# Half products dealt between the last units of attention, and the order of small sums on VectorE, in a GNN and attention kernel

## The chip, the cores and the metric

The kernel runs on one core of one Trainium2 chip. The metric is the device time of one execution in microseconds (us), the median of three runs. The profile is that of one further execution.

## What is computed

Node features x (1024 x 512) pass a layer norm and a relu, then a graph convolution, four transformer layers and a second graph convolution. The layers are nearly all of the time:

```
for i in range(L):                       # L = 4
    a = _attn(_ln(h, ln2), cond, Wq[i], Wk[i], Wv[i], Wo[i])
    h = h + a
    u = _ln(h, ln3) @ geglu_w[i] + geglu_b[i]          # 512 -> 4096
    val, gate = jnp.split(u, 2, axis=-1)
    f = val * gelu(gate)
    h = h + f @ ffo_w[i] + ffo_b[i]                    # 2048 -> 512
# _attn: 16 batches; 64 queries (rows of h) and 256 keys and values (from cond) each, 8 heads of 64
```

## The kernel before

Each of the five engines has its own instruction list, written out by hand in Python functions; nothing is scheduled by a program. Order between engines is kept by semaphores: `x.wait_ge(sem, value)` in front of an instruction, `.then_inc(sem, 1)` behind one. A waiting instruction holds up all that stands behind it on its engine. TensorE is `pe` (PE in the profile), VectorE `dve` (DVE), ScalarE `act` (ACT), GpSimd `pool` (POOL).

**Split products.** Every float32 product is three matmuls: upper by upper part, upper by lower, lower by upper. The upper part of a tile is a rounded copy, made mostly by ScalarE (`..._high`), the lower part the rest, a subtraction on VectorE or GpSimd (`..._low`). `product` (L2347 to L2349) issues these three per piece of 128 rows; four pieces (KC) make a product of 12 matmuls.

**A layer's attention.** The 1024 rows are 8 groups of 128 (t = 0 to 7), two batches each. Per group, keys and values are each made by a seven-product scheme: `kv_step(t, kind, j)`, j = 0 to 6, 12 matmuls of 256 columns each (L2596 to L2599), into three PSUM banks. VectorE combines them: `kv_two` (L1977), `kv_five` (L1985, the "fifth step's sum"), `kv_late(.., 0 to 2)` (L2000). Step 4 waits for `kv_five`, step 6 for `kv_late(.., 1)` by

```
elif j == 6:
    pe.wait_ge(kv_sum, 5 * n + 4)
```

Each group has four units u (two heads each). A unit is `s_product` (scores), `maxima` (L2050), `exp_of`, `softmax` (the reciprocal, L2056), `normalise`, `p_transpose` (L2624), `pT_high` and `pT_low` (L2061), `pv_product` (L2643 to L2648) and `o_part` (L2038, sums halves of its result out of the one bank that the next `pv_product` needs). `value_units(t)` interleaves the values of group t with its first two units, `key_units(t)` the keys of group t + 1 with its last two. `o_low` (L2044) makes the lower part for the output product `wo_product(t - 1)`, whose result `residual` (L2068) adds to h; norm statistics follow, the reciprocal root on GpSimd (`rsqrt`), `z3_of` (L2075), four transposes on TensorE (`t3`, L2692), `x3_full` (ScalarE, L1295), `x3_high` (L1304) and `x3_low` (L2088 on VectorE, L866 on GpSimd): the input of the second half of the layer. In layer 0 ScalarE and GpSimd also split the conditioning blocks of the next group (`cond_block`, `cond_low`); step j of the keys waits for block j.

**Front of a layer.** The first four query tiles (use 0, then use 1) go through `first_t2` (transposes), `first_x2_full` (L2006), `first_x2_high` (ScalarE), `first_x2_low` (L2015) and `q_product(use, p)`, with the seven key steps of group 0 in between.

**End of the attention.** The last group has no keys to make. Products of the second half's first four steps (s = 0 to 3, value and gate v = 0, 1; `mlp_product(0, 0, s, v, r)`) are put in their place. A half product takes the first 256 or the last 256 of the 512 columns: tiles 0, 1 or 2, 3 of x3 (of tiles 4 to 7 for s = 2, 3). Step s = 3 uses the banks of s = 1. After step s comes `gelu(s)` on ScalarE and `mlp_step(s)` (L2197) on VectorE, which raises `ff_ok`. Then come `full_product` (L2716 to L2720) and the rest of the layer, in which TensorE doesn't stop.

## Time and profile before

| | us |
|---|---|
| three runs | 2416.61, 2417.24, 2417.92 |
| median | 2417.24 |
| profiled execution | 2417.82 |
| its span | 2416.0 |
| TensorE busy (14270 matmuls) | 2331.7 (97%) |
| VectorE busy | 1635.8 (68%) |
| ScalarE busy | 1244.2 (51%) |
| GpSimd busy | 1050.1 (43%) |
| chain that ended last: TensorE, VectorE, ScalarE, GpSimd | 78%, 10%, 7%, 2% |

Times in the rows are microseconds from the start of the span. Matmuls overlap: one of 256 columns lasts 0.28 us from its start to its end, but the next starts long before. Layer 0 begins at about 178 us; the shown rows are mostly of layer 2 (1275 to 1828 us), as layers 1 to 3 repeat to a tenth of a microsecond.

### The profile page before, as it was taken

What the parts mean: (1) busy time and instruction counts of PE and PEld (TensorE: products, weight loads), DVE (VectorE), ACT (ScalarE), POOL (GpSimd) and SP (SyncE); (2) the same over time, 40 slices, a digit from 0 to 9 for tenths busy, and PEclk for the clock granted to TensorE, in tenths of its full rate; (3) what the DMA queues carried; (4) which work ended last, traced back from release to release, by engine and by line L of the source; (5) the groups of instructions that cost most, each with busy time, mean ns of one, the idle gap of its engine ahead of it and who ended that gap; (6) DMA issues with size and microseconds to landing.
All of it is one profiled execution on the core that took longest, in us unless ns stands there. A gap on an engine that the chain in (4) does not pass through costs nothing.

```text
span 2416.0 us, 38420 instructions
## 1 busy us (share of the span) xinstructions
PE 2331.7 (97%) x14270; PEld 2047.1 (85%) x14270; DVE 1635.8 (68%) x3043; ACT 1244.2 (51%) x2585; POOL 1050.1 (43%) x714
## 2 busy tenths in 40 slices
PE   7898999999999999999999999999999999999999
PEld 5358898988888999988888999988888999888887
DVE  9975667686656666686656666686656666685554
ACT  9954666654333555654433555653333555553322
POOL 3126766646643322356542322356652322355530
PEclk9899999999999999999999999999999999999999
DMA  2033333312221433312231333312231333212230
GB/s 79 1 137 126 134 146 126 129 40 66 61 92 72 127 104 118 97 44 63 63 123 52 122 103 109 97 44 70 62 118 69 119 106 104 87 53 63 63 128 35
DMA packets 115880, 214.53 MB, mean 89 GB/s; under 512 B 9520, under 2 KB 71600, under 8 KB 113904
## 3 DMA queue, kind: packets, MB, share of 16 engines
q1 hardware_dynamic: 115408, 207.89, 26.2%
q10 hardware_dynamic: 288, 4.19, 0.4%
q8 instruction: 115, 1.88, 0.3%
q14 instruction: 69, 0.57, 0.1%
HBM read 176.13 MB, written 35.91 MB: 88 GB/s over the span
## 4 chain that ended last, share of the span: by engine, by line
PE 78%; DVE 10%; ACT 7%; issue 3%; POOL 2%; DMA 0%; DVEq 0%; SPq 0%; ACTq 0%; POOLq 0%
PE ps L2347 9%; PE ps L2348 9%; PE ps L2349 9%; PE ps L2596 8%; PE ps L2599 7%; PE ps L2598 7%; PE ps L2716 7%; PE ps L2720 7%; PE ps L2718 7%; PE ps L2624 2%; ACT z L1295 2%; PE ps L2646 1%; DVE oh_d L1698 1%; PE ps L2910 1%; PE ps L2648 1%
## 5 line engine op out<-in xcount | busy, mean ns | idle before, releaser
L2596 PE MATMUL ps<-cb,wk_hi 128*128 128x256 f32 x896 | 260.0, 290 | 18.4 <-DVE kv L2000 11.7
L2596 PE MATMUL ps<-wv_hi,cb 128*128 128x256 f32 x896 | 257.7, 288 | 8.9 <-DVE kv L1985 5.0
L2599 PE MATMUL ps<-cb,wk_lo 128*128 128x256 f32 x896 | 255.4, 285 | 0.0
L2598 PE MATMUL ps<-cb,wk_hi 128*128 128x256 f32 x896 | 255.4, 285 | 0.0
L2599 PE MATMUL ps<-wv_hi,cb 128*128 128x256 f32 x896 | 253.4, 283 | 0.0
L2598 PE MATMUL ps<-wv_lo,cb 128*128 128x256 f32 x896 | 253.4, 283 | 0.0
L874 POOL TENSOR_TENSOR f_lo<-ff,f_hi 128x512 fp32r<-128x512 f32 x128 | 169.0, 1333 | 171.2 <-ACT f_hi L1499 171.1
L823 POOL TENSOR_TENSOR v_lo<-kv,v_hi 128x512 fp32r<-128x512 f32 x96 | 124.5, 1298 | 257.5 <-ACT v_hi L1253 257.5
L2282 DVE TENSOR_TENSOR h<-h,ps 128x512 f32<-128x512 f32 x256 | 169.1, 683 | 65.4 <-PE ps L2349 64.8
L2347 PE MATMUL ps<-wf_hi,f_hi 128*128 128x512 f32 x512 | 199.2, 389 | 0.0
L2348 PE MATMUL ps<-wf_lo,f_hi 128*128 128x512 f32 x512 | 199.2, 389 | 0.0
L2349 PE MATMUL ps<-wf_hi,f_lo 128*128 128x512 f32 x512 | 199.2, 389 | 0.0
L2000 DVE TENSOR_TENSOR kv<-ps,kv 128x512 f32<-128x512 f32 x192 | 132.4, 690 | 90.6 <-PE ps L2599 86.8
L2596 PEld LDWEIGHTS ps<-cb,wk_hi 128*128 128x128 f32 x896 | 173.4, 194 | 23.7 <-DVE kv L2000 9.3
L2716 PE MATMUL ps<-xT_hi,wg_hi 128*128 128x512 f32 x480 | 187.2, 390 | 0.1
L2720 PE MATMUL ps<-xT_hi,wg_lo 128*128 128x512 f32 x480 | 186.8, 389 | 0.0
L2718 PE MATMUL ps<-xT_lo,wg_hi 128*128 128x512 f32 x480 | 186.7, 389 | 0.0
L2596 PEld LDWEIGHTS ps<-wv_hi,cb 128*128 128x128 f32 x896 | 171.5, 191 | 13.0 <-DVE kv L1985 6.8
L823 POOL TENSOR_TENSOR kT_lo<-kv,kT_hi 128x512 fp32r<-128x512 f32 x96 | 124.0, 1293 | 117.5 <-ACT kT_hi L1253 108.3
L2598 PEld LDWEIGHTS ps<-cb,wk_hi 128*128 128x128 f32 x896 | 173.8, 194 | 1.1
L2599 PEld LDWEIGHTS ps<-cb,wk_lo 128*128 128x128 f32 x896 | 173.6, 194 | 0.0
L2598 PEld LDWEIGHTS ps<-wv_lo,cb 128*128 128x128 f32 x896 | 171.7, 192 | 0.0
(376 smaller groups left out, 6886.1 us busy)
## 6 DMA issues: line engine op xcount, KB each, us to landing
cb<-cb_s SPq DMA_DIRECT2D x168, 512.0 KB, 4.6
stage<-in_pieces SPq DMA_DIRECT2D x256, 128.0 KB, 2.6
cb_s<-cb SPq DMA_DIRECT2D x56, 512.0 KB, 2.6
stage<-in_pieces SPq DMA_DIRECT2D x44, 512.0 KB, 3.7
stage<-in_condT SPq DMA_DIRECT2D x7, 1024.0 KB, 5.9
stage<-in_pieces SPq DMA_DIRECT2D x16, 256.0 KB, 3.3
at_s<-at_hi ACTq DMA_DIRECT2D x2, 2048.0 KB, 12.9
wo_raw<-in_pieces SPq DMA_DIRECT2D x8, 512.0 KB, 4.5
```

What stands on the lines that cost most here:

```text
L823: pool.tensor_tensor(kv_place(1, kind, *KV_LATER[n]), kv_temp(n), bits(kv_place(0, kind, *KV_LATER[n])), ALU.subtract).then_inc(kv_ok, 1)
L874: pool.tensor_tensor(f_lo[q % 2][:, c, half * HALF:(half + 1) * HALF], ff[:, s % 2, :], bits(f_hi[q % 2][:, c, half * HALF:(half + 1) * HA ...
L2282: dve.tensor_tensor(h[:, t, :], h[:, t, :], ps[:, down_bank(q, t), :], ALU.add)\
L2347: pe.matmul(bank, l_hi, r_hi, start=(first and i == 0), stop=False)
L2348: pe.matmul(bank, l_hi, r_lo, start=False, stop=False)
L2349: end = pe.matmul(bank, l_lo, r_hi, start=False, stop=(last and i == n - 1))
L2596: pe.matmul(to, l_hi, r_hi, start=(fresh and i == 0 and k == 0), stop=False, skip_group_check=True)
L2598: pe.matmul(to, l_hi, r_lo, start=False, stop=False, skip_group_check=True)
L2599: last = pe.matmul(to, l_lo, r_hi, start=False, stop=(k == 1), skip_group_check=True)
L2716: pe.matmul(ps[:, bank, :], hi[:, a, r], moving[0][:, n, :], start=(first and n == 0), stop=False, skip_group_check=True)
L2718: pe.matmul(ps[:, bank, :], hi[:, a, r], moving[1][:, n, :], start=False, stop=False, skip_group_check=True)
L2720: last = pe.matmul(ps[:, bank, :], lo[:, a, r], moving[0][:, n, :], start=False, stop=(n == 1), skip_group_check=True)
```

## The change

Instructions change places within their engines' lists; in addition two lower parts of x3 per layer (tiles 0 and 1) go from GpSimd (two instructions each) to VectorE (one each), and 36 matmuls per layer are added, since three products of 512 columns are issued as two of 256. Nothing is left out and no buffer is added. By part:

- Front of a layer: `q_product` takes a list of pieces and for p = 0 waits for one lower part of x2 per piece; `q_product(1, 0)` gives its first piece before key step 6. On VectorE `kv_late(0, KEYS, 1)` comes after the first lower part and the full part of tile 2.
- Groups: on VectorE `kv_five` comes before `q_low` in both halves of a group, `o_low` before the reciprocal. On ScalarE `q_high(t + 1, 0)` comes ahead of the conditioning blocks. For t = 0 `kv_late(.., 1)` of the values comes before the reciprocal.
- Last group and the start of the second half: other places for the half products on TensorE, with other waits; upper parts of x3 one or two units earlier on ScalarE (`x3_high(0)` after `pT_high(u)`, `x3_high(1)` at its old place, and in `key_units` `x3_full(5)`, `x3_high(2)`, `x3_high(3)` before `pT_high(u)`, `x3_high(4)` and `x3_high(5)` before `pT_high(u + 1)`); lower parts 0 and 1 among the value sums of group 7; `gelu(0)` before `x3_full(6)`; `mlp_step(0)` before `x3_low(6)`.

The diff without the parts on ScalarE and GpSimd that the list above gives in full (indentation cut):

```diff
@@ -1360,16 +1349,14 @@
...
             if last:
-                x3_high(0)
+                x3_high(1)
             if ahead:
...
                 o_high(GROUPS * l + t - 1)
-            if last:
-                x3_high(1)
-            elif t > 1:
+            if t > 1 and not last:
                 x3_full(t - 2)
@@ -1380,16 +1367,18 @@
...
             normalise(u)
+            if not last:
+                q_high(t + 1, 0)
             if ahead:
...
             if not last:
-                q_high(t + 1, 0)
                 kv_11_high(t + 1, KEYS)
             else:
+                x3_full(5)
                 x3_high(2)
-                x3_full(5)
+                x3_high(3)
             pT_high(u)
@@ -1402,13 +1391,11 @@
...
             else:
-                x3_high(3)
                 x3_high(4)
+                x3_high(5)
             pT_high(u + 1)
...
                 kv_high(t + 1, KEYS, 2)
-            else:
-                x3_high(5)
@@ -1516,9 +1503,9 @@
...
+        gelu(0)
         x3_full(6)
         x3_high(6)
-        gelu(0)
         down_high(0)
@@ -2096,35 +2083,45 @@
...
             if t:
-                q_low(t, 1)
                 o_part(u - 2, 2)
             kv_five(t, VALUES)
+            if t:
+                q_low(t, 1)
             kv_11_low(t, VALUES)
...
             kv_late(t, VALUES, 0)
+            if t == 0:
+                kv_late(t, VALUES, 1)
             softmax(u + 1)
-            kv_late(t, VALUES, 1)
             if t:
+                kv_late(t, VALUES, 1)
                 o_part(u - 1, 3)
+            if t == GROUPS - 1:
+                x3_low(0)
             kv_late(t, VALUES, 2)
+            if t == GROUPS - 1:
+                x3_low(1)
             maxima(u + 2)
+            if t == GROUPS - 1:
+                o_low(GROUPS * l + t - 1)
             pT_low(u + 1)
...
             u, last = UNITS * l + PAIRS * t + 2, t == GROUPS - 1
-            if last:
+            if t and not last:
                 o_low(GROUPS * l + t - 1)
             softmax(u)
-            if t and not last:
-                o_low(GROUPS * l + t - 1)
             if not last:
...
             if not last:
+                kv_five(t + 1, KEYS)
                 q_low(t + 1, 0)
-                kv_five(t + 1, KEYS)
+            else:
+                x3_low(2)
+                x3_low(3)
             if t:
@@ -2140,8 +2137,6 @@
...
             if last:
-                x3_low(2)
-                x3_low(3)
                 o_part(u, 2)
@@ -2169,13 +2164,12 @@
...
             first_x2_full(1, k)
-        for k in T2_ORDER[1][:2]:
+        first_x2_low(1, 0)
+        first_x2_full(1, 2)
+        kv_late(0, KEYS, 1)
+        for k in T2_ORDER[1][1:]:
             first_x2_low(1, k)
-        first_x2_full(1, 2)
-        for k in T2_ORDER[1][2:]:
-            first_x2_low(1, k)
-        for n in range(1, 3):
-            kv_late(0, KEYS, n)
+        kv_late(0, KEYS, 2)
         q_low(0, 0)
@@ -2292,11 +2286,11 @@
...
         add_bias(NT - 2)
+        mlp_step(0)
         x3_low(NT - 2)
...
         z3_of(NT - 1, GROUPS * l + NT - 1)
-        mlp_step(0)
         t_sums(0, (3,))
@@ -2665,17 +2659,22 @@
...
-        def q_product(use, p):
-
-            if p == 0:
-                pe.wait_ge(x2_ok, 2 * FIRST * l + FIRST * use + FIRST)
+        def q_product(use, p, places=range(KC)):
+
             if p == 0 and use == 0:
...
             r = slice(p * P, (p + 1) * P)
-            product(ps[:, FIRST_BANK[p], :], [(wq_hi[:, k, r], wq_lo[:, k, r], xT2_hi[:, k, :], xT2_lo[:, k, :])
-                                              for k in range(KC)]).then_inc(q_mm, 1)
+            for i in places:
+                k = T2_ORDER[use][i]
+                if p == 0:
+                    pe.wait_ge(x2_ok, 2 * FIRST * l + FIRST * use + i + 1)
+                last = product(ps[:, FIRST_BANK[p], :],
+                               [(wq_hi[:, k, r], wq_lo[:, k, r], xT2_hi[:, k, :], xT2_lo[:, k, :])],
+                               i == 0, i == KC - 1)
+            if places[-1] == KC - 1:
+                last.then_inc(q_mm, 1)
@@ -2805,33 +2804,37 @@
...
             pv_product(u - 2, t, 0)
+            if last:
+                pe.wait_ge(kv_sum, 5 * (kv_set(l, t, VALUES) + 1))
+                pe.wait_ge(w_ok, FIRST_PIECES + PIECES * l + 2)
+                pe.wait_ge(x3_ok, 2 + NT * l + 2)
+                mlp_product(0, 0, 0, 1, slice(0, 2 * P))
             if t:
...
                 kv_step(t + 1, KEYS, 3)
-            else:
-                pe.wait_ge(w_ok, FIRST_PIECES + PIECES * l + 2)
-                pe.wait_ge(x3_ok, 2 + NT * l + 2)
-                pe.wait_ge(full3_ok, NT * l + 6)
-                mlp_product(0, 0, 0, 0, slice(0, 2 * P))
             p_transpose(u)
...
                 kv_step(t + 1, KEYS, 5)
+            else:
+                pe.wait_ge(full3_ok, NT * l + 6)
+                mlp_product(0, 0, 0, 0, slice(0, 2 * P))
             pv_product(u - 1, t, 1)
...
             else:
-                mlp_product(0, 0, 0, 1, slice(0, 2 * P))
+                mlp_product(0, 0, 1, 0, slice(0, 2 * P))
                 pv_product(u, t, 2)
-                pe.wait_ge(x3_ok, 2 + NT * l + 4)
-                mlp_product(0, 0, 0, 0, slice(2 * P, HALF))
             p_transpose(u + 1)
...
             else:
+                mlp_product(0, 0, 1, 1, slice(0, 2 * P))
+                pe.wait_ge(x3_ok, 2 + NT * l + 4)
+                mlp_product(0, 0, 0, 1, slice(2 * P, HALF))
                 pv_product(u + 1, t, 3)
@@ -2845,9 +2848,11 @@
...
         first_t2(1, T2_ORDER[1][3:])
-        for j in range(5, BLOCKS):
-            kv_step(0, KEYS, j)
-        for p in range(PAIRS):
+        kv_step(0, KEYS, 5)
+        q_product(1, 0, range(1))
+        kv_step(0, KEYS, 6)
+        q_product(1, 0, range(1, KC))
+        for p in range(1, PAIRS):
             q_product(1, p)
@@ -2873,25 +2878,27 @@
...
+        mlp_product(0, 0, 0, 0, slice(2 * P, HALF)).then_inc(u_mm, 1)
         pe.wait_ge(o_part_ok, 2 + UNITS * l + UNITS - 1)
         t3(6)
-        mlp_product(0, 0, 0, 1, slice(2 * P, HALF)).then_inc(u_mm, 1)
-        mlp_product(0, 0, 1, 0, slice(0, 2 * P))
+        mlp_product(0, 0, 1, 0, slice(2 * P, HALF))
+        mlp_product(0, 0, 1, 1, slice(2 * P, HALF)).then_inc(u_mm, 1)
         wo_product(GROUPS * l + GROUPS - 1)
-        mlp_product(0, 0, 1, 0, slice(2 * P, HALF))
-        mlp_product(0, 0, 1, 1, ks=range(0, 3))
-        t3(7)
-        mlp_product(0, 0, 1, 1, ks=range(3, KC)).then_inc(u_mm, 1)
...
         mlp_product(0, 0, 2, 1, slice(0, 2 * P))
+        t3(7)
+
+        pe.wait_ge(ff_ok, 32 * l + 2)
+        for v in range(2):
+            mlp_product(0, 0, 3, v, slice(0, 2 * P))
         pe.wait_ge(x3_ok, 2 + NT * l + NT)
-        mlp_product(0, 0, 2, 0, slice(2 * P, HALF))
-        mlp_product(0, 0, 2, 1, slice(2 * P, HALF)).then_inc(u_mm, 1)
-        mlp_step(0, 0, 3)
+        for s in range(2, 4):
+            mlp_product(0, 0, s, 0, slice(2 * P, HALF))
+            mlp_product(0, 0, s, 1, slice(2 * P, HALF)).then_inc(u_mm, 1)
         full_product()
```

How the instructions stand, by engine. VectorE in `key_units` of a group with t from 1 to 6; the qbd rows are the query lower parts, L1985 (L1972 in the changed kernel) is the fifth step's sum, the rows from `wo_mm` down the residual and its norm statistics. Before:

```order
L2056 RECIPROCAL rinv<-rsum 128x2 [waits exp_ok]
L2044 TENSOR_TENSOR oT_lo<-o_full,oT_hi 128x512 [waits o_hi_ok]
L1977 TENSOR_TENSOR kv<-ps,kv 128x512 [waits kv_p1,step_mm]
L2038 TENSOR_REDUCE o_full<-ps 64x128 [waits o_ok,pv_mm]
L2038 TENSOR_REDUCE o_full<-ps 64x128
L2023 TENSOR_TENSOR qbd_a<-z,qbd_a 64x4x64 [waits qb_hi_ok]
L2023 TENSOR_TENSOR qbd_a<-z,qbd_a 64x4x64
L1985 TENSOR_TENSOR kv<-ps,kv 128x512 [waits kv_sum,step_mm]
L2068 TENSOR_TENSOR h<-h,ps 128x512 [waits wo_mm]
L1600 BN_STATS stats<-h 128x6 [waits h_att]
L1603 BN_AGGR mv<-stats 128x2 [waits ln]
L1606 TENSOR_SCALAR veps<-mv 128x1 [waits ln]
```

and in the changed kernel:

```order
L2031 TENSOR_TENSOR oT_lo<-o_full,oT_hi 128x512 [waits o_hi_ok]
L2043 RECIPROCAL rinv<-rsum 128x2 [waits exp_ok]
L1964 TENSOR_TENSOR kv<-ps,kv 128x512 [waits kv_p1,step_mm]
L2025 TENSOR_REDUCE o_full<-ps 64x128 [waits o_ok,pv_mm]
L2025 TENSOR_REDUCE o_full<-ps 64x128
L1972 TENSOR_TENSOR kv<-ps,kv 128x512 [waits kv_sum,step_mm]
L2010 TENSOR_TENSOR qbd_a<-z,qbd_a 64x4x64 [waits qb_hi_ok]
L2010 TENSOR_TENSOR qbd_a<-z,qbd_a 64x4x64
L2055 TENSOR_TENSOR h<-h,ps 128x512 [waits wo_mm]
L1587 BN_STATS stats<-h 128x6 [waits h_att]
L1590 BN_AGGR mv<-stats 128x2 [waits ln]
L1593 TENSOR_SCALAR veps<-mv 128x1 [waits ln]
```

The two query lower parts went from ahead of the fifth step's sum to behind it, and `o_low` (oT_lo) from behind the reciprocal to ahead of it.

TensorE in the second half's first steps, at the transposes of the last tile (`t3(7)`, ident,z). Before, they stand inside a product of step 1 of 512 columns, and `mlp_step(1)`'s `ff_ok` is waited for only before step 3. The transposes:

```order
L2347 MATMUL ps<-xT_hi,w_hi 128x512
L2348 MATMUL ps<-xT_lo,w_hi 128x512
L2349 MATMUL ps<-xT_hi,w_lo 128x512
L2692 MATMUL ps<-ident,z 128x128 [waits z3_ok]
L2692 MATMUL ps<-ident,z 128x128 x3
L2347 MATMUL ps<-xT_hi,w_hi 128x512
L2348 MATMUL ps<-xT_lo,w_hi 128x512
L2349 MATMUL ps<-xT_hi,w_lo 128x512
L2347 MATMUL ps<-xT_hi,w_hi 128x256 [waits x3_ok]
```

and, 48 matmuls of 256 columns later, the start of step 3:

```order
L2348 MATMUL ps<-xT_lo,w_hi 128x256
L2349 MATMUL ps<-xT_hi,w_lo 128x256
L2347 MATMUL ps<-xT_hi,w_hi 128x512 [waits ff_ok]
L2348 MATMUL ps<-xT_lo,w_hi 128x512
L2349 MATMUL ps<-xT_hi,w_lo 128x512
```

In the changed kernel the wait for `ff_ok` stands right behind them:

```order
L2341 MATMUL ps<-xT_hi,w_hi 128x256
L2342 MATMUL ps<-xT_lo,w_hi 128x256
L2343 MATMUL ps<-xT_hi,w_lo 128x256
L2691 MATMUL ps<-ident,z 128x128 [waits z3_ok]
L2691 MATMUL ps<-ident,z 128x128 x3
L2341 MATMUL ps<-xT_hi,w_hi 128x256 [waits ff_ok]
L2342 MATMUL ps<-xT_lo,w_hi 128x256
L2343 MATMUL ps<-xT_hi,w_lo 128x256
```

The products of steps 1 and 2 that stood between the transposes and the wait have moved ahead of the transposes or behind step 3's first halves.

## Rows read from the trace of the kernel before

**Rows 1.** The profile's page: the span.

```profile
span 2416.0 us, 38420 instructions
```

**Rows 2.** TensorE waits, whole span: line, releaser: us total, times, longest.

```profile
PE ps L2596 <- DVE kv L2000: 15.6, 8, 3.0
PE ps L2347 <- DVE oT_lo L2044: 10.2, 24, 1.1
PE ps L2596 <- DVE kv L1985: 8.4, 7, 3.5
PE ps L2643 <- DVE pT L2061: 5.6, 4, 1.4
...
PE ps L2596 <- POOL cb L803: 3.3, 6, 0.9
...
PE ps L2347 <- ACT z L1295: 2.3, 4, 0.6
...
PE ps L2643 <- DVE o_full L2038: 2.1, 4, 0.5
...
PE ps L2347 <- DVE xT_lo L2088: 1.6, 4, 0.4
```

**Rows 3.** TensorE timeline, front of layer 2: start, duration, operation [idle before].

```profile
1285.92 0.50 PE L2347 MATMUL ps<-xT_hi,wq_hi 128*128 128x512 f32 x1 [0.60 <-DVE xT_lo L2015]
...
1299.96 0.28 PE L2598 MATMUL ps<-cb,wk_hi 128*128 128x256 f32 x1
1300.08 0.28 PE L2599 MATMUL ps<-cb,wk_lo 128*128 128x256 f32 x1
1303.26 0.58 PE L2596 MATMUL ps<-cb,wk_hi 128*128 128x256 f32 x1 [2.90 <-DVE kv L2000]
```

**Rows 4.** TensorE, five longest stops: stretch, length, busy (count), clock, DMA.

```profile
203.00:215.00 12.00, 9.01 (x46) 0.86 0.00 1
243.00:255.00 12.00, 8.54 (x58) 0.86 0.60 220
760.00:772.00 12.00, 9.10 (x53) 1.00 0.01 1
1299.00:1311.00 12.00, 9.10 (x39) 0.72 0.00 0
1841.00:1853.00 12.00, 9.10 (x43) 0.86 0.01 2
```

**Rows 5.** Timeline of VectorE, keys of a middle group of layer 2.

```profile
1464.03 0.85 DVE L2023 TENSOR_TENSOR qbd_b<-z,qbd_b 64x256 fp32r<-64x256 f32 x2
1467.17 0.69 DVE L1985 TENSOR_TENSOR kv<-ps,kv 128x512 f32<-128x512 f32 x1 [2.29 <-PE ps L2599]
...
1472.65 0.69 DVE L2000 TENSOR_TENSOR kv<-ps,kv 128x512 f32<-128x512 f32 x1
```

**Rows 6.** Timeline of TensorE in the same group: output product, key step 6.

```profile
1462.69 0.50 PE L2347 MATMUL ps<-wo_hi,oT_hi 128*128 128x512 f32 x1 [0.30 <-DVE oT_lo L2044]
...
1473.39 0.39 PE L2596 MATMUL ps<-cb,wk_hi 128*128 128x256 f32 x1
```

**Rows 7.** Timelines of VectorE, ScalarE and TensorE, start of layer 2's second half.

```profile
1579.61 0.69 DVE L2068 TENSOR_TENSOR h<-h,ps 128x512 f32<-128x512 f32 x1 [0.41 <-PE ps L2349]
...
1587.02 0.75 DVE L2197 SCALAR_TENSOR_TENSOR ff<-ps,cols_sb,gel 128x512 f32<-128x512 f32 x1 [0.26 <-ACT gel L1449]
...
1583.64 1.51 ACT L1295 ACTIVATE z<-ps,cols_sb 128x128 f32<-128x128 f32 x4 [1.78 <-PE ps L2692]
...
1595.03 0.39 PE L2349 MATMUL ps<-xT_hi,w_lo 128*128 128x512 f32 x1
1595.26 0.39 PE L2716 MATMUL ps<-xT_hi,wg_hi 128*128 128x512 f32 x1
```

**Rows 8.** Timelines of VectorE and GpSimd, a middle group of layer 0.

```profile
328.04 2.96 DVE L2023 TENSOR_TENSOR qbd<-z,qbd 64x256 fp32r<-64x256 f32 x2
...
327.65 1.64 POOL L798 TENSOR_TENSOR t_s<-stage,t_s 128x512 f32<-128x512 f32 x1
```

More of the change, by code:

```diff
@@ L859, in _ @@
             for l in range(L):
-                def x3_low(t):
-                    r = slice(t % 4 * P, (t % 4 + 1) * P)
-                    pool.wait_ge(x3_hi_ok, NT * l + t + 1)
-                    for ks in (slice(0, 2), slice(2, KC)):
-                        last = pool.tensor_tensor(xT3_lo[t // 4][:, ks, r],
-                                                  z3[:, t, :].rearrange("p (k n) -> p k n", n=P)[:, ks, :],
-                                                  bits(xT3_hi[t // 4][:, ks, r]), ALU.subtract)
-                    last.then_inc(x3_ok, 1)
                 def f_low(q, s, half, c):
@@ L941, in value_units @@
                         cond_low(g, 3)
-                    if last:
-                        x3_low(0)
-                        x3_low(1)
                 def key_units(t):
@@ L1355, in value_units @@
                     pT_high(u)
+                    if last:
+                        x3_high(0)
                     exp_of(u + 1)
@@ L2116, in key_units @@
                     u, last = UNITS * l + PAIRS * t + 2, t == GROUPS - 1
-                    if last:
+                    if t and not last:
                         o_low(GROUPS * l + t - 1)
                     softmax(u)
-                    if t and not last:
-                        o_low(GROUPS * l + t - 1)
                     if not last:
@@ L2807, in key_units @@
                     pv_product(u - 2, t, 0)
+                    if last:
+                        pe.wait_ge(kv_sum, 5 * (kv_set(l, t, VALUES) + 1))
+                        pe.wait_ge(w_ok, FIRST_PIECES + PIECES * l + 2)
+                        pe.wait_ge(x3_ok, 2 + NT * l + 2)
+                        mlp_product(0, 0, 0, 1, slice(0, 2 * P))
                     if t:
```

## The prediction

> **What bounds the kernel now.** The page first: one core, span 2416.0 us [rows 1]. The profiled execution took 2417.82 us, of which 1.8 us lie around the span; it is 0.6 us above the median of the three runs, 2417.24. The sum below is a difference, so I add it to the median. A measurement of this kernel tells about 0.2% (4.8 us) from no change.
>
> Then the waits of TensorE over the whole span [rows 2]. Everything after the graph stage is a chain of matmuls, and what the change can give is the time in which TensorE stands still. Per layer these are few and repeat exactly: two at the front of the attention stage, one before each output product, a handful around the last group. The timeline of TensorE gives the price of a matmul back to back: 0.12 us at 256 columns [rows 3], 0.23 us at 512 [rows 7]. A half product (12 matmuls of 256) costs 1.44 us, a whole one 2.72 us, so dealing one whole as two halves costs 0.16 us. Last, the granted clock around the longest stops [rows 4]: of five stops, four are followed by a stretch at 1.2 instead of 2.4 GHz. The loss is (1 - clock) x 12 us: 1.7, 1.7, 0, 3.4 and 1.7 us, in all 8.5 us.
>
> **The change, part by part.**
>
> *Front of a layer, first query product.* It waits for all four lower parts of x2 (0.60 us idle) [rows 3]. Now it starts on the first; 0.6 idle and 0.15 of broken overlap go: 0.75 us in each of four layers, **-3.0**.
>
> *Front, key step 6.* TensorE stops 2.90 us before it [rows 3] because `kv_late(0, KEYS, 1)` stands on VectorE behind all lower parts of x2. Now that sum comes after one lower part and one transposed tile, and TensorE has three matmuls of the query product in between. VectorE then ends the sum about 2.75 us sooner, and TensorE waits 0.2 us: 2.75 in layers 1 to 3, **-8.3**, and their clock comes back, 3.4 + 1.7, **-5.0** [rows 4]. In layer 0, GpSimd still has to make the lower parts of the value weights and then of the next conditioning blocks, which follow a transfer; they let TensorE gain less. Bounds: 1.0 (that chain doesn't move) and 4.5 (all of it and the 1.7 of clock). I take **-2.2**, nearer to the lower end because the chain hangs on GpSimd work that moves little.
>
> *The fifth key step's sum ahead of the query lower parts.* This is the part that cuts both ways.
> In layer 0 the sum waits for query upper parts that ScalarE makes behind three conditioning blocks; the seven stops on L1985 are 8.4 us, 3.5 of it one stop [rows 2]. The long one is exchanged for a wait on the next sum: of 3.5 + 1.7 clock I count 3.2. Of the six others (5.0 us plus first-matmul losses) nearly all, 4.9. Together **-8.1**; bounds 4 and 11.
> In the groups t = 1 to 6 of every layer it costs. Before, the two lower-part instructions (0.88 us from start to start of the next) ran in 2.29 us in which VectorE waited for key step 2 [rows 5]. Now they stand behind the fifth step's sum, and from there VectorE has no gap: residual, statistics, `kv_11_low`, maxima, `pT_low`, `z3_of`, two more sums, until `kv_late(.., 1)` starts at 1472.65 and ends at 1473.34. Key step 6 needs it and starts at 1473.39 [rows 6], 0.05 us later, which is where it would start anyway. So the slack is about 0.1 us and the rest of 0.88 appears as a stop of TensorE: about 0.8 us in 18 groups. In layer 0 the same delay moves the residual, hence the reciprocal root on GpSimd, hence the lower parts of block 5, for which TensorE already waits (3.3 us in six stops) [rows 2]: 0.88 in six groups. **+19.7**. Bounds: 0 if the chain had slack, 24 x 0.98 if it had none and the first matmul is slow. I take it near the upper end, since the rows show start and end of the chain 0.05 us apart.
>
> *Output product.* It stops 0.3 us in groups 2 to 6 of each layer (20 of the 24 stops in 10.2 us) [rows 2, 6], as `o_low` stood behind the reciprocal. Now it stands ahead. With the broken overlap and the slow first matmul (0.50 instead of 0.40) I count 0.55 each: **-11.2**.
>
> *Last group and what follows.* Before, the stops there are 1.05 for oT_lo, 1.4, 0.6, 0.5 and 0.4: 4.0 us per layer [rows 2]. More half products are put between the units, and three whole products are split (36 extra matmuls, 0.5 us). Walking the changed order by the durations of the timeline, TensorE gets eight half products rather than five before the last output product, but the third product of values waits for `o_part`, which on VectorE now stands behind two lower parts of x3 that wait for ScalarE. If everything moved to VectorE ran alone, the last output product would end 0.7 us later than before for 4.3 us more work done.
> Then comes the step I weigh most. Half products of step 3 are put behind `t3(7)`, and wait for `ff_ok` 2, because steps 1 and 3 share banks. That value is written by `mlp_step(1)`. Its chain is unchanged: last output product, residual (1579.61), norm, `t3(7)`, `x3_full(7)` (starts 1583.64), upper part, gelu(1), `mlp_step(1)` (1587.02 + 0.75 = 1587.77) [rows 7]: 8.2 us. Before, TensorE had 11.2 us of other work behind `t3(7)`. Now only two half products stand between the output product and `t3(7)`, and nothing behind it, so TensorE stops from the end of the transposes (+4.0) to +8.2: **a new stop of 4.2 us per layer**. Six half products (8.7 us) follow, so the full product starts 16.9 us after the output product's end; before it was 1595.26 - 1579.61 = 15.7 [rows 7]. So +1.2, and with the 0.7 +1.9 per layer.
> Two of the moved instructions, `x3_low(0)` and `o_low`, now fall beside GpSimd's lower parts of v. The query lower parts show what that does: two take 0.85 us alone and 2.96 us beside GpSimd [rows 5, 8], 1.05 us more each. I count 0.9 for each of the two, since each delays what follows on VectorE: +1.8 per layer. Together 3.7 x 4 = **+14.8**; bounds 1.4 and 5 per layer.
> The Trainium skill (SBUF — State Buffer, section "SBUF: two separate sides") says more strictly that a VectorE instruction with two SBUF inputs and a GpSimd instruction exclude each other for their whole length, and whichever starts first keeps the other out. By that rule the moved `x3_low(0)` would wait for nearly all of a GpSimd subtraction; the row agrees with such a wait, its size per instruction being 1.05 us. Without that rule and that row the 1.8 would be 0.
>
> *Clock at the new stop.* No row has a stop of 4.2 us. The nearest, 2.9 to 3.5 us, lost 1.7 on average and 2.1 where they lost any [rows 4]. Being longer than all of these, I give it 2.1 each: **+8.4**; bounds 0 and 3.4 each.
>
> **Sum.** Gains 3.0 + 8.3 + 5.0 + 2.2 + 8.1 + 11.2 = 37.8. Costs 19.7 + 14.8 + 8.4 = 42.9. Net +5.1 us, 2422.3.
>
> **The rivals.**
> (a) *The VectorE chain after the fifth sum is not the limit.* If key step 6 starts on time in spite of the moved lower parts, 19.7 us go: 2402.6, faster. It decides once the chain has over 0.8 us of slack. For it: no stop of TensorE shows there now. Against: 0.05 us between the sum's end and the step [rows 5, 6].
> (b) *The stop after t3(7) is short.* If gelu(1) or the residual comes earlier than the old chain says, so that TensorE waits 2 us or less and keeps its clock, 4 x 2.2 + 8.4 go: 2405, faster. Against: every link of the chain has its old place behind `t3(7)`.
> (c) *No collisions with GpSimd.* Then 7.2 us go: 2415, no change. For it: half a microsecond of shift decides who starts first.
> (d) *The clock falls more often.* The two-microsecond wait before the third product of values, or a remainder in layer 0, add a slow stretch per layer as in the worst row (3.4 instead of 2.1), or the front's drops stay: +8 to +9, 2431.
>
> **How the numbers follow.** Forecast 0.5 (own range 2415 to 2429), (a) 0.1, (b) 0.1, (c) 0.15, (d) 0.15. Faster by over 0.2%: (a) and (b), 0.2. Same (2412.4 to 2422.1): (c) and a good third of the forecast, as 2422.3 lies on its edge, 0.35. Slower: 0.45. The range leaves out (a) and (b) and reaches down to 2411, under (c) and the forecast's own range, and up to (d): 2411 to 2431.
>
> **What would show it.** In the trace after: no stop of 2.9 us at the front of a layer and no slow clock there; no stop before the output products of groups 2 to 6; instead 24 stops of about 0.8 us at key step 6 (in layer 0, at step 5, 1.3 us); in each layer one stop of about 4.2 us behind the last transposes, released by the product of values and gelu on VectorE, with the clock at 1.2 GHz behind it in most layers; `x3_low(0)` or `o_low` ending about 1 us late beside GpSimd. Total idle before half products under 3 us per layer, or key step 6 without stops, would prove me wrong.

## The result, and the profile after

The changed kernel takes **2435.5 us** (median of 4 runs, 2432.8 to 2437.6) against 2417.0 of the kernel before on the same chip: ratio 1.0075, 95% interval 1.0062 to 1.0088. It is 18.5 us slower; the prediction said 5.1 slower, with a range that ended at 2431. The sign was right and every stop that was foretold is there; one place was overlooked, and the time lies outside the range.

The page of the changed kernel, its span and the busy times of the engines:

```profile
span 2433.5 us, 38716 instructions
...
PE 2337.2 (96%) x14414; PEld 2064.2 (85%) x14414; DVE 1662.9 (68%) x3051; ACT 1243.1 (51%) x2585; POOL 1038.4 (43%) x698
```

TensorE is busy 5.5 us more (before 2331.7), the span is 17.5 us longer. The waits of TensorE over the whole span (line, releaser: us in total, times, longest), against [rows 2]:

```profile
PE ps L2590 <- DVE kv L1987: 23.8, 35, 1.6
PE ps L2341 <- DVE ff L2191: 17.2, 4, 4.3
PE ps L2590 <- POOL cb L803: 8.8, 7, 1.4
PE ps L2637 <- DVE o_full L2025: 7.7, 4, 2.0
...
PE ps L2590 <- POOL wv_lo L782: 3.0, 1, 3.0
```

L1987 is `kv_late` (L2000 before): its longest stop has fallen from 3.0 to 1.6, but there are 35 of them instead of 8. The 10.2 us before the output products and the 8.4 on the fifth sum are gone. The 4.3 us stops on `ff_ok` 2 are there. Timeline of TensorE in layer 2 (start, duration, operation, in brackets the idle time before it and its releaser): key step 6 of the layer's front, key step 6 of a middle group, value step 6 of group 7, the third product of values of group 7, the first half product of step 3, the full product.

```profile
1310.18 0.39 PE L2590 MATMUL ps<-cb,wk_hi 128*128 128x256 f32 x1 [0.20 <-DVE kv L1987]
...
1477.85 0.39 PE L2590 MATMUL ps<-cb,wk_hi 128*128 128x256 f32 x1 [0.62 <-DVE kv L1987]
...
1559.61 0.39 PE L2590 MATMUL ps<-wv_hi,cb 128*128 128x256 f32 x1 [1.57 <-DVE kv L1987]
...
1576.02 0.35 PE L2637 MATMUL ps<-pT,v_hi 128*128 128x256 f32 x1 [1.97 <-DVE o_full L2025]
...
1598.68 0.58 PE L2341 MATMUL ps<-xT_hi,w_hi 128*128 128x256 f32 x1 [4.31 <-DVE ff L2191]
...
1610.00 0.40 PE L2715 MATMUL ps<-xT_hi,wg_hi 128*128 128x512 f32 x1
```

The 2.90 us at the front [rows 3] are 0.20 now. The third row is one that the prediction does not have. Its cause is on VectorE and GpSimd, same stretch:

```profile
1551.25 0.69 DVE L1972 TENSOR_TENSOR kv<-ps,kv 128x512 f32<-128x512 f32 x1 [0.31 <-PE ps L2593]
1551.86 4.52 DVE L2010 TENSOR_TENSOR qbd<-z,qbd 64x256 fp32r<-64x256 f32 x2
...
1558.88 0.68 DVE L1987 TENSOR_TENSOR kv<-ps,kv 128x512 f32<-128x512 f32 x1
```

```profile
1551.10 5.00 POOL L732 TENSOR_TENSOR w_lo<-stage,w_hi 128x1024 fp32r<-128x1024 f32 x2 [3.32 <-ACT w_hi L1298]
```

The two query lower parts of the last group, `q_low(7, 1)`, moved behind the fifth sum, run beside GpSimd's lower parts of the second half's weights (`up_low`) and take 4.52 us instead of 0.85. All that is queued behind them on VectorE is 3.7 us late, `kv_late(7, VALUES, 1)` too, for which value step 6 waits. In the kernel before, the same two lower parts (VectorE) had ended 0.16 us before GpSimd began (the second row is GpSimd):

```profile
1545.27 0.85 DVE L2023 TENSOR_TENSOR qbd<-z,qbd 64x256 fp32r<-64x256 f32 x2
...
1546.28 4.81 POOL L732 TENSOR_TENSOR w_lo<-stage,w_hi 128x1024 fp32r<-128x1024 f32 x2 [3.32 <-ACT w_hi L1311]
```

The granted clock in windows of 12 us around the stops (stretch, length, busy of each engine, then the clock as a share of 2.4 GHz, DMA share, GB/s): step 3 of layer 1; layer 2's value step 6, third product of values, and step 3; step 3 of layers 3 and 0.

```profile
1050.00:1062.00 12.00, 8.90 (x54) 8.90 (x55) 10.34 (x8) 5.33 (x11) 9.21 (x5) 0.72 0.29 87
1558.00:1570.00 12.00, 10.43 (x65) 9.86 (x65) 8.31 (x16) 9.18 (x25) 4.23 (x3) 0.86 0.13 37
1576.00:1588.00 12.00, 11.98 (x87) 11.91 (x88) 5.78 (x10) 5.79 (x12) 0.00 (x0) 0.86 0.01 1
1597.00:1609.00 12.00, 10.32 (x64) 10.32 (x65) 11.68 (x10) 4.70 (x9) 9.21 (x5) 0.72 0.29 87
...
2139.00:2151.00 12.00, 8.26 (x52) 8.26 (x53) 10.17 (x8) 5.73 (x12) 9.13 (x5) 0.72 0.29 86
...
505.00:517.00 12.00, 9.48 (x61) 9.48 (x62) 10.91 (x9) 5.36 (x10) 9.22 (x5) 0.72 0.31 88
```

A window at 0.86 holds 3.4 us at 1.2 GHz, one at 0.72 holds 6.8 (they differ from 1 by half the time at 1.2 GHz). Added over the layers (178 us to the end), the changed kernel's TensorE is at 1.2 GHz for 54 us, that of before for 17 [rows 4]; at half speed that costs at most 27 us against 8.5. It is less where TensorE stands still in part of the stretch: compared with matmuls at full clock, and with layers whose clock stays up, a stretch costs 2.1 to 2.7 us behind the 4.3 us stop, 1.2 behind the stop at value step 6 (from there to the third product of values 16.2 to 16.6 us in layers 1 to 3, 15.3 in layer 0) and 1.5 behind the stop before that product (from there to step 3 22.7 us in layers 0 to 2, 21.2 in layer 3).

### The profile page after: what moved, and what is told of

It reads as the page before. It is cut to its first block, busy times and chain, and to the rows that moved or that the text cites. A ratio compares the mean times of both kernels' runs of the same rounds, so it can differ in the third digit from the quotient of the medians.

```text
span 2433.5 us, 38716 instructions
## 1 busy us (share of the span) xinstructions
PE 2337.2 (96%) x14414; PEld 2064.2 (85%) x14414; DVE 1662.9 (68%) x3051; ACT 1243.1 (51%) x2585; POOL 1038.4 (43%) x698
## 4 chain that ended last, share of the span: by engine, by line
PE 78%; DVE 14%; issue 3%; ACT 3%; POOL 2%; DMA 0%; DVEq 0%; SPq 0%; ACTq 0%; POOLq 0%
PE ps L2341 9%; PE ps L2342 9%; PE ps L2343 9%; PE ps L2719 7%; PE ps L2715 7%; PE ps L2717 7%; PE ps L2590 7%; PE ps L2593 7%; PE ps L2592 7%; PE ps L2618 2%; PE ps L2640 1%; DVE oh_d L1685 1%; PE ps L2642 1%; PE ps L2917 1%; DVE kv L1987 1%
## 5 line engine op out<-in xcount | busy, mean ns | idle before, releaser
L2590 PE MATMUL ps<-wv_hi,cb 128*128 128x256 f32 x896 | 259.0, 289 | 14.3 <-DVE kv L1987 11.3
L2590 PEld LDWEIGHTS ps<-cb,wk_hi 128*128 128x128 f32 x896 | 171.4, 191 | 30.2 <-DVE kv L1987 16.5
L2590 PEld LDWEIGHTS ps<-wv_hi,cb 128*128 128x128 f32 x896 | 173.6, 194 | 18.0 <-DVE kv L1987 13.7
L1987 DVE TENSOR_TENSOR kv<-ps,kv 128x512 f32<-128x512 f32 x192 | 131.5, 687 | 76.2 <-PE ps L2593 73.2
L1308 ACT ACTIVATE p_exp<-ps,nmx 128x256 f32<-128x256 f32 x256 | 119.4, 474 | 122.4 <-DVE nmx L2037 122.2
L2593 PEld LDWEIGHTS ps<-wv_hi,cb 128*128 128x128 f32 x896 | 174.0, 194 | 0.0
```

The costliest lines, as they stand in the source:

```text
L1987: dve.tensor_tensor(wide(kv_temp(which)), ps[:, bank, :], wide(other[:, :, :]), ALU.add)\
L2590: pe.matmul(to, l_hi, r_hi, start=(fresh and i == 0 and k == 0), stop=False, skip_group_check=True)
L2593: last = pe.matmul(to, l_lo, r_hi, start=False, stop=(k == 1), skip_group_check=True)
```

## The experiments

**Parts of the change, alone and in sums.** Differences are of medians; those between kernels that were measured at different times carry about 1 us of uncertainty (the medians of the kernel before, measured each time beside them, lie between 2416.7 and 2418.1).

*b_front*: before, with the three edits at the front of a layer (`q_product` by pieces, its first piece before key step 6, `kv_late(0, KEYS, 1)` behind the first lower part), as in the diff above.

> The kernel before with the change at the front of a layer alone (q_product piece by piece, its first piece ahead of key step 6, kv_late(0, KEYS, 1) behind the first lower part). Theory: the prediction's terms for the front are right as they stand: 3.0 (first query product) + 8.3 (key step 6 in layers 1 to 3) + 5.0 (their clock) + 2.2 (layer 0) = 18.5, so about 2398.5, and the 1.2 GHz stretches at 1302 and 1845 are gone. Rival: the clock falls anyway at the front, 5 us less: 2403.5. Rival: the gain is used up by a later wait of the same layer (the scores of the first unit): 3 us or less of it stay, 2413.

2401.8 us, ratio 0.9939 (0.9926 to 0.9953): -14.9, between theory and first rival. Both slow stretches at 1302 and 1845 are gone; layers 1 to 3 have none. Layer 0 gains little, as it now stops 3.0 us for GpSimd's lower parts of the value weights.

*b_olow*: before, with

```diff
-                    softmax(u)
                     if t and not last:
                         o_low(GROUPS * l + t - 1)
+                    softmax(u)
```

> The kernel before with o_low ahead of the reciprocal in the groups 1 to 6 alone. Theory: the 0.3 us stops before the output products of groups 2 to 6 go, 20 x 0.55 = 11 us: 2406. Rival: only the idle time itself counts, 20 x 0.3 = 6 us: 2411. Rival: the reciprocal comes 0.7 us later, and normalise, p_transpose and the third score product with it; TensorE stops there instead: no change, 2417.

2407.7 us, 0.9957 (0.9943 to 0.9970): -9.1, and no stop before the output products of groups 2 to 6. From the first output product of layer 2 to that of tile 6 the trace shows 189.7 us instead of 192.5: 2.8 per layer, 0.56 for each of five stops. In the trace the theory holds, at the size predicted. The medians say 2 us less than the 11.2 of four such layers; the interval holds both.

*c_front_olow* is both, *c_l0* adds, in layer 0 alone, `kv_five` before `q_low` in groups 0 to 6, `q_high(t + 1, 0)` ahead of the conditioning blocks, and `kv_late(0, VALUES, 1)` ahead of the reciprocal.

> The kernel before with two parts of the change: the front of a layer and o_low ahead of the reciprocal. Alone they gave -14.9 and -9.1. Theory: independent places, so they add: -24, 2393. Rival: they share the clock (both end slow stretches), 3 us less: 2396.

> As the kernel with the front and o_low, and in layer 0 alone also the new order of kv_five and q_low (VectorE, groups 0 to 6, both halves), q_high(t + 1, 0) ahead of the conditioning blocks, and kv_late(0, VALUES, 1) ahead of the reciprocal. Theory: the prediction's two terms for layer 0, -8.1 for the stops on the fifth sum and +5.3 for key step 5 (six stops now 1.33 us against 0.55 before), make -2.8 against the kernel without it. Rival: the wait of 3.0 us for the value weights' lower parts stays ahead in both, the long stop isn't exchanged but only moved: 0 to +2.

2391.6 us (0.9891, 0.9875 to 0.9908): they add. 2390.0 us (0.9886, 0.9870 to 0.9903): -1.7 for layer 0, between theory and rival. The stops on the fifth sum are replaced by 1.3 us each at key step 5:

```profile
PE ps L2608 <- POOL cb L803: 8.0, 6, 1.3
PE ps L2608 <- DVE kv L2003: 7.8, 14, 1.9
```

*d_no_end* has front, `o_low` and the new order of `kv_five` in all layers, and the end of the attention as before; *e_q71_old* is the same but for

```diff
+                    if t == GROUPS - 1:
+                        q_low(t, 1)
                     if t:
                         o_part(u - 2, 2)
                     kv_five(t, VALUES)
-                    if t:
+                    if 0 < t < GROUPS - 1:
                         q_low(t, 1)
```

> The changed kernel with the last group's and the second half's part undone: front, o_low, kv_five ahead of q_low in all layers stay. It sizes the query lower parts in layers 1 to 3 without the end stage behind them, against 2390.0 of the kernel that has them late in layer 0 alone. Theory: 18 stops of 0.61 us, 0.74 each with what the first matmul loses (the prediction had 0.8), and the same collision with GpSimd's lower part of w in group 7 of layers 1 to 3, which makes a stop of 1.5 us at value step 6 and costs 1.7 us of clock or none: 13 + 5 to 10, so 2408 to 2413. Rival: GpSimd begins L732 later in this order (x3_low(0) and x3_low(1) follow it there), the collision does not happen, 13 us alone: 2403.

> The kernel without the end part (2411.5), only q_low(7, 1) at its exact old place, ahead of o_part(u - 2, 2). Theory: the excess over 13.3 us (18 stops of 0.61, 0.74 each) is this collision: 1.77 us per layer in all four layers, and whatever clock follows (3.4 us here): the stops of 1.55 to 1.58 at value step 6 go, 2401 to 2404. Rival: the excess is spread over the groups or is clock that falls elsewhere in the layer: 2408 or more.

2411.5 us (0.9977, 0.9967 to 0.9986) and 2402.3 us (0.9940, 0.9927 to 0.9954). TensorE's waits for `kv_late` in the two:

```profile
PE ps L2599 <- DVE kv L2001: 23.7, 35, 1.6
```

```profile
PE ps L2601 <- DVE kv L2001: 17.6, 31, 1.0
```

One call at its old place, in each of four layers, takes away four stops, 6.1 us of waiting and 9.2 us of time. The rest is clock: TensorE is at 1.2 GHz for 14 us in d_no_end, 7 of them in layer 2 at value step 6, and for 7 us in e_q71_old. What is left over c_l0 is 12.3 us, for the 18 stops of 0.61. The rows of e_q71_old (VectorE, GpSimd) show that the collision is gone:

```profile
1533.34 0.84 DVE L2024 TENSOR_TENSOR qbd<-z,qbd 64x256 fp32r<-64x256 f32 x2
```

```profile
1534.34 4.81 POOL L732 TENSOR_TENSOR w_lo<-stage,w_hi 128x1024 fp32r<-128x1024 f32 x2 [3.32 <-ACT w_hi L1311]
```

So the excess is the collision in group 7; both rivals (no collision without the end part; a loss spread over the groups) fall.

*b_end*: before, with the last group's and the second half's part alone.

> The kernel before with the last group's and the second half's part of the change alone (half products, their waits, x3 upper and lower parts, gelu(0), mlp_step(0)); front, kv_five, q_low and o_low of the groups as before. Theory: this part alone loses what the prediction undersized: the stop of 4.3 us on ff_ok 2 with 6.8 us at 1.2 GHz behind it (3 us), the stop of 2.0 us before the third product of values with 3.4 us at 1.2 GHz (1.7 us) in two or three layers, +0.7 us of sequence: about 7 us in each of 4 layers, 2440 to 2446, the stop of 1.55 us at value step 6 not being there. Rival: the prediction's own terms, 14.8 + 8.4 = 23: 2440 or less with only 1.7 to 2.1 us of clock per layer. Rival: this part is worth nothing by itself and the loss in the changed kernel comes from the query lower parts: 2420.

2440.3 us (1.0093, 1.0078 to 1.0108): +23.5. On top of the other parts it costs the same: 2435.5 - 2411.5 = 24.0. The wait rows of this kernel:

```profile
PE ps L2338 <- DVE ff L2188: 17.2, 4, 4.3
...
PE ps L2634 <- DVE o_full L2024: 8.0, 4, 2.0
```

The two stops belong to the end's rearrangement; the loss in the changed kernel does not come from the query lower parts alone, as the last rival had it. The total lies on the edge between the theory and the first rival and doesn't part them; the trace does, for the theory: 6.8 us at 1.2 GHz follow each 4.3 us stop, 3.4 us three of the four 2.0 us stops.

**Single waits undone in the changed kernel.** *a_gelu1*:

```diff
                 x3_high(6)
+                gelu(1)
                 down_high(0)
...
                 f_high(0, 0, 0, 0)
-                gelu(1)
...
                 residual(NT - 1, GROUPS * l + NT - 1)
+                mlp_step(1)
                 z3_of(NT - 1, GROUPS * l + NT - 1)
...
                 x3_low(NT - 1)
-                mlp_step(1)
```

> The changed kernel, only gelu(1) on ScalarE moved from behind x3_high(7) to behind x3_high(6), and mlp_step(1) on VectorE from behind x3_low(7) to between the residual of tile 7 and z3_of. Theory: in the changed kernel step 1's products end before the last output product (1587.4), and TensorE stops 4.3 us for ff_ok 2 only because gelu(1) still stands behind x3_full(7) (1597.1); the slow clock behind that stop is its consequence. Then the stop on ff_ok is gone, at most 0.7 us are left before the second halves (x3_low(7)), the full product starts about 13 us after the residual instead of 19.5, the 1.2 GHz stretches behind it (6.8 us long) go: 6.5 us in each of 4 layers, -26 against the changed kernel, about 2409. Rival 1: the clock falls for another reason (the dense half products); the stretch stays and only 3.6 us per layer go: about 2421. Rival 2: the step on VectorE delays z3_of and t3(7), and the wait moves there: 2 us per layer, about 2427.

2418.4 us (1.0005, 0.9996 to 1.0014): -17.0 against the changed kernel, 26 expected. The first rows are the changed kernel, ScalarE and VectorE in layer 2:

```profile
1594.51 1.51 ACT L1282 ACTIVATE z<-ps,cols_sb 128x128 f32<-128x128 f32 x4 [1.91 <-PE ps L2691]
...
1597.10 0.67 ACT L1436 ACTIVATE gel<-ps,cols_sb 128x512 f32<-128x512 f32 x1
...
1597.88 0.75 DVE L2191 SCALAR_TENSOR_TENSOR ff<-ps,cols_sb,gel 128x512 f32<-128x512 f32 x1 [0.25 <-ACT gel L1436]
```

and these a_gelu1's, ScalarE, VectorE and TensorE:

```profile
1579.81 0.67 ACT L1436 ACTIVATE gel<-ps,cols_sb 128x512 f32<-128x512 f32 x1
...
1583.73 0.75 DVE L2191 SCALAR_TENSOR_TENSOR ff<-ps,cols_sb,gel 128x512 f32<-128x512 f32 x1
...
1589.02 0.39 PE L2341 MATMUL ps<-xT_hi,w_hi 128*128 128x256 f32 x1 [0.44 <-DVE xT_lo L2075]
```

Its window behind the transposes, with the clock at 1.00:

```profile
1588.00:1600.00 12.00, 11.00 (x72) 9.83 (x72) 11.66 (x9) 4.47 (x9) 9.27 (x5) 1.00 0.31 89
```

Here `mlp_step(1)` runs in the gap in which VectorE waits for the reciprocal root, ahead of z3. The stop and the slow clock behind it are gone in all four layers. The full product starts 16.7 us after the output product's start instead of 22.5. Up to it the theory holds in the main (5.8 us per layer, 6.5 expected). But 1.9 of these are given back behind it: the full product's first matmul on `w_hi` starts 30.9 us after the output product instead of 34.8. The cause is the first of two waits that the expectation did not have:

```profile
PE ps L2715 <- POOL wg_lo L897: 5.1, 4, 1.3
...
PE ps L2715 <- POOL wg_lo L894: 2.2, 4, 0.6
```

GpSimd starts its lower parts only after `x3_low(7)`, and they are the next to be late.

*a_x3low*:

```diff
                     else:
-                        x3_low(2)
-                        x3_low(3)
...
                     o_part(u - 1, 1)
                     if last:
+                        x3_low(2)
+                        x3_low(3)
                         o_part(u, 2)
```

> The changed kernel, only x3_low(2) and x3_low(3) of the last group on VectorE moved from ahead of the residual to behind o_part(u - 1, 1). Theory: VectorE waits 2.4 us for their upper parts with the residual, the maxima and o_part queued behind them, which makes TensorE's 2.0 us stop before the third product of values. Without it that stop goes in all layers, and the 3.4 us at 1.2 GHz behind it where it stands (layers 1 and 2): 4 x 1.9 + 2 x 1.7 = 11 us, about 2424.5. Rival: the two lower parts are now the late ones, and the wait moves to the half product of step 0 on tiles 2 and 3, about 1 us per layer left: about 2428.

2420.3 us (1.0014, 1.0005 to 1.0023): -15.2. The residual starts 1.9 to 2.7 us sooner behind the last sum of the values (layers 1 to 3) and the stop before the third product of values is gone, without one in its place. The gain is above the 11 expected: the time at 1.2 GHz falls by 17 us, where 6.8 were expected, also behind the later stop.

*a_q71* puts `q_low(7, 1)` ahead of `kv_five`, one call later than its place before the change (behind `o_part(u - 2, 2)`).

> The changed kernel, only the query lower parts of the last group's values (q_low(7, 1)) put back ahead of kv_five, as before the change. Theory: the two run 4.5 us instead of 0.85 because GpSimd's lower part of w (L732) has started; that delays kv_late(1) and makes the 1.55 us stop at value step 6, and the 1.2 GHz stretch of 3.4 us right behind it in layers 1 to 3 is its consequence. Then both go: 4 x 1.5 + 3 x 1.7 = 11 us, about 2424. Rival: the stretch has another cause; only 6 us go, about 2429. Other rival: the two lower parts were late anyway and the stop comes back at the scores: no change.

2427.5 us (1.0044, 1.0030 to 1.0058): -8.0. GpSimd starts at 1547.14 there, 0.1 us after the two lower parts, which take 2.98 us:

```profile
1547.02 2.98 DVE L2010 TENSOR_TENSOR qbd<-z,qbd 64x256 fp32r<-64x256 f32 x2
```

```profile
1547.14 5.13 POOL L732 TENSOR_TENSOR w_lo<-stage,w_hi 128x1024 fp32r<-128x1024 f32 x2 [3.31 <-ACT w_hi L1298]
```

So the collision was only shortened; 0.5 us of wait at value step 4 stays, and other short waits of the last group grow. In the group nearly as much is waited as before (the 1.55 us stops, 6.2 us, are gone, and 5.2 us of other waits came). The time at 1.2 GHz falls from 54 to 34 us, so most of the gain is clock.

*a_qlow*:

```diff
                     if not last:
+                        if l:
+                            q_low(t + 1, 0)
                         kv_five(t + 1, KEYS)
-                        q_low(t + 1, 0)
+                        if l == 0:
+                            q_low(t + 1, 0)
```

> The changed kernel, only q_low(t + 1, 0) on VectorE put back ahead of kv_five in the keys of layers 1 to 3 (layer 0 keeps the new order, and so do the values). Theory: the VectorE chain from the fifth sum to kv_late(.., 1) has no slack; the 18 stops of 0.61 us at key step 6 go, 18 x 0.7 = 12 to 13 us, about 2423, with the output products still without a stop. Rival: other work on VectorE (o_low ahead of the reciprocal) keeps part of the stops: 0.3 us each stay, about 2429.

2418.2 us (1.0004, 0.9995 to 1.0013): -17.3. The 18 stops are gone (the row for `kv_late` falls from 35 stops to 17), the output products still have none. The 4 us above the expectation fit the clock: 44 instead of 54 us at 1.2 GHz. The stops of 1.55 us at value step 6 are still there, but no slow stretch follows them, where one did in each of layers 1 to 3; what is gone is a stop of 0.61 us, 16.5 us ahead of each.

**The repaired kernel.** *best1* is the changed kernel with these four edits. *best2* adds two, *best3* also the exact old place of `q_low(7, 1)`:

```diff
-                for t in (NT - 2, NT - 1):
-                    rsqrt(GROUPS * l + t)
-                wait_apart(pool, x3_ok, 2 + NT * l + NT)
+                rsqrt(GROUPS * l + NT - 2)
+                wait_apart(pool, x3_ok, 2 + NT * l + NT - 1)
                 down_low(0)
+                rsqrt(GROUPS * l + NT - 1)
+                wait_apart(pool, x3_ok, 2 + NT * l + NT)
...
+                weight_sums(1, 1)
                 mlp_step(2)
-                weight_sums(1, 1)
```

> The changed kernel with all four single edits together: gelu(1) and mlp_step(1) early, q_low(7, 1) ahead of kv_five, x3_low(2) and x3_low(3) behind o_part(u - 1, 1), q_low of the keys ahead of kv_five in layers 1 to 3. The edits alone gave -17.0, -8.0, -15.2 and -17.3 against the changed kernel's 2435.5. Theory: the stops are separate and add up, the clock less than singly since all of it (54 us of 1.2 GHz, 27 us of time) can be won once only: -50 to -57, 2378 to 2386. Rival: GpSimd's lower parts of the gate weights, for which TensorE already waits 1.8 us per layer once the full product comes early, take up what comes on top: 2395.

> The changed kernel with the four single edits together, and two more: GpSimd makes the lower part of the down weights (down_low(0)) after x3_low(6) and before the last tile's reciprocal root, rather than after x3_low(7), and VectorE makes the weight sums of set (1, 1) before mlp_step(2). Theory: with the stop on ff_ok gone, TensorE's 0.55 + 1.29 us in the full product wait for GpSimd's lower parts of the gate weights; started 2.6 us and 2 us earlier they are there in time, and 1.8 us in each of 4 layers go: 2383.5. Rival: GpSimd now runs beside the residual and the norm of the last tile on VectorE and holds it up as the query lower parts were held up; t3(7) comes 1 to 3 us later: 2391 or more.

> The repaired kernel of 2387.2 with q_low(7, 1) at its exact old place, ahead of o_part(u - 2, 2). Theory: at the later place it still ran beside GpSimd's lower part of w (2.98 us for two instead of 0.85) and left stops of 0.49 and 0.50 us per layer; at the old place it runs before GpSimd starts and both go: -1.0 to -1.3 us in each of 4 layers, 2382 to 2383. Rival: the 0.50 us before the half product is the lower part of x3 tile 1 and stays: 2385.

2390.6 (0.9891, 0.9876 to 0.9906), 2387.2 (0.9876, 0.9859 to 0.9892) and **2384.8 us** (0.9868, 0.9853 to 0.9883). best1 is 44.8 below the changed kernel, less than the 57.5 of the four edits singly: the clock can be won back once only. Singly the four edits took away 85 us at 1.2 GHz in sum, together only 48, and layers 1 to 3 have none left. The rival's GpSimd wait does not explain the gap: it is 7.3 us as in a_gelu1, and so already in the 57.5. best2 removes the 0.55 us stop but not the 1.25 us one, and t3(7) comes 0.3 us later: half of the expected gain. best3 gains 2.5 us where 4 to 5 were expected: the half product's 0.50 us stays, as its rival said. best3 beats both kernels, by 33 and by 51 us. But c_l0, which keeps the old end of the attention, is at 2390.0: of the 33 us at most 5 are owed to the dealt half products, and best2's edits on GpSimd and VectorE are in them; the rest is the front, `o_low` and layer 0.

## Why the prediction was wrong, point by point

The steps of the sum, in the order in which the kernels add them:

| | predicted | measured | from |
|---|---|---|---|
| front and `o_low` | -29.7 | -25.3 | 2417.0 to c_front_olow |
| layer 0, both terms | -2.8 | -1.7 | to c_l0 |
| query lower parts of layers 1 to 3, without `q_low(7, 1)` | +14.4 | +12.3 | to e_q71_old |
| `q_low(7, 1)` in the last group | none | +9.2 | to d_no_end |
| last group and its clock | +23.2 | +24.0 | to the changed kernel |
| sum | +5.1 | +18.5 | |

**The step that failed** is the part on the fifth key step's sum ahead of the query lower parts. It walks through "the groups t = 1 to 6" at key step 6 and layer 0's step 5, and costs the moved calls there. The same edit also moves `q_low(7, 1)`, in values of the last group, where the list of GpSimd differs: it alone has `up_low` there. The prediction priced this kind of collision, 1.05 us per instruction [rows 5, 8], for `x3_low(0)` and `o_low`, and did not look for it at this call. It cost 9.2 us, two thirds of the miss. The timeline of before would have shown it: `q_low(7, 1)` ended 0.16 us before GpSimd's L732 began. The collision made a stop of 1.55 to 1.58 us in each layer, at value step 6, and let the clock fall behind it.

**The gains were taken too large** by 4.4 + 1.1 us. This is less sure than the 9.2: the interval of c_front_olow alone reaches from 22 to 30 us of gain. The stops went as predicted (0.20 us at the front, none before the output products, the first query product without a wait). What the front gives is 17.2 us between the two profiled spans but 14.9 between medians, where 18.5 were taken. The 5.0 of clock was read from one execution, and executions of the kernel before alone spread by 7 us (2413.3 to 2420.4 in 27 runs) with their clock. Even in that execution it is 4.4: from the 2.90 us stop to the next one TensorE takes 23.9 us in layer 1, where the clock stays up, and 26.7 and 25.5 in layers 2 and 3. For the output products 20 x 0.55 is 11.0, not the 11.2 of the sum. And in layer 0 a stop of 3.0 us for the lower parts of the value weights came in the place of the one removed.

**Key step 6**: right in mechanism, a stop of 0.61 us where 0.8 was taken; with what the first matmul loses it is 12.3 us over 18 groups, 0.69 each. Rival (a), slack on VectorE, is refuted. **Layer 0**: 1.33 us instead of 1.3 at key step 5, as predicted.

**Last group**: the stop of 4.2 us is one of 4.31, released as predicted; rival (b) is refuted in this kernel. a_gelu1 shows that it was avoidable: step 1's last product now ends before the output product of tile 7 starts, and only `gelu(1)` and `mlp_step(1)` had kept their old places. The "11.2 us of other work behind `t3(7)`" was a misreading, though no term hangs on it: it counts step 3, which itself waits for `ff_ok`; in the trace of before step 3 starts at 1589.79, 2.0 us after `mlp_step(1)` ends. The total, 23.2, is nearly exact by luck: with the costs of a slow stretch above, the clock took about 14 us (9.4 behind the four 4.3 us stops and 3 x 1.5) where 8.4 stood, which leaves about 10 for all the rest, where 14.8 stood. Counted too much: the two collisions, which are 0.43 and 0.66 us (`x3_low(0)` 1.12, `o_low` 1.35 instead of 0.69) where 0.9 each was taken; so rival (c) was half right here. In b_end, where GpSimd's timing differs, `x3_low(0)` takes 1.75 us, 1.07 more than alone. Counted too little: the clock. Behind the 4.3 us stop it costs 2.7 us in layer 2 (the 72 matmuls from 1598.68 to 1610.00 take 11.3 us, at 0.12 each they are 8.6) and 2.1 to 2.4 in the others, where 2.1 were taken: little is missing here. More is missing behind the 2.0 us stop before the third product of values: 1.5 us in three layers, where nothing was taken.

**Rival (d)** named this last mechanism and was the nearest. Its 2431 was too low since it had the front's and the last group's drops, but not the third place, value step 6, with a stop and a slow stretch of its own. Counted as half the time at 1.2 GHz, the clock costs up to 27 us in the profiled execution where it cost up to 8.5 before; the prediction's terms made it 10.

**The rule and the row.** The prediction set the Trainium skill's rule (SBUF — State Buffer, section "SBUF: two separate sides") beside a row: of a VectorE instruction with two SBUF inputs and a GpSimd instruction that reads SBUF, the one that starts first keeps the other out for its whole length. The new rows agree with it better than with a fixed price: beside GpSimd instructions of 1.5 to 1.6 us each query lower part is 1.05 us longer [rows 8], beside those of 2.5 us (L732, 5.00 for two) 1.8 us longer (4.52 for two), while the fifth sum with a PSUM input (1551.25, 0.69 us) is not longer at all beside the same instruction.

## What to carry to other kernels

A reorder inside a unit that a loop repeats has to be followed at the loop's last and first turns apart: what stands on the other engines there is not what stands in a middle turn, and here one call in the last turn of each layer cost 9.2 us in all, the 18 in the middle turns 12.3. Where work is moved ahead on one engine, look for the links of its chain on the others that kept their places: putting `gelu(1)` and `mlp_step(1)` where their inputs were ready took a 4.3 us stop away, and the engine that was next to be late, GpSimd, took 1.9 us of the gain. And measure the parts of a compound change apart: of this one two parts win 25 us and two lose 46.

## What was not expected of the hardware

The price of a stop lies in the granted clock as well as in its length, and length alone does not decide whether the clock falls: the three stops of 2.90 us in the kernel before were followed by 0, 6.8 and 3.4 us at 1.2 GHz [rows 4]. In the five profiled kernels with the 4.3 us stop (changed, b_end, a_q71, a_x3low, a_qlow) TensorE is at 1.2 GHz behind all 20 of them, for 3.4 or 6.8 us. Of the 20 stops of 1.66 to 2.0 us before the third product of values (changed, b_end, a_gelu1, a_q71, a_qlow), 11 are followed by a slow stretch: 3 of 4 in the changed kernel, none of 4 in a_q71, where the stop of 1.55 us some 16 us earlier is gone. Of the 20 stops of 1.54 to 1.58 us at value step 6 (changed, a_gelu1, a_x3low, a_qlow, d_no_end), 9 are followed by one: 3 of 4 in the changed kernel, none of 4 in a_qlow, where the stop of 0.61 us some 16 us earlier is gone in three layers. In c_l0 and best1, with no stop above 1.41 us in layers 1 to 3, no slow stretch is in these layers. What decides between such stops is left open; that removing one stop can also free the clock behind another (a_x3low, a_qlow) is what the runs show.
